# One attention step's products in another order: all attention products first, then all linear products, and x1's rest ahead of the first gated sum

## The chip, the cores and the metric

The kernel runs on one core of one Trainium2 chip. The metric is the time of one execution on the device in microseconds (us); lower is better. The core's engines are TensorE (PE in the rows, PEld its weight loads), VectorE (DVE), ScalarE (ACT), GpSimd (POOL) and SyncE (SP), which issues transfers. Each has its own queue of instructions, and they meet only at semaphores.

## The reference

Two layers over x, 8 x 512 tokens of 256 features, in 32-bit floats. The change is in the first, a gated attention unit. For each of the 8 sequences of 512 tokens:

- x is normed; qk = silu(x Wqk), v = silu(x Wv) (512 wide), gate = silu(x Wg) (512 wide).
- From qk come four sets of heads, turned by position: two queries and two keys.
- **Attention part**: within groups of 64 tokens, att = relu(q k / 64 + bias) squared, and quad_out = att v.
- **Linear part**: kv = k2 v over the whole sequence, divided by 512, and lin_out = q2 kv.
- out = gate * (quad_out + lin_out), then the output projection Wo, a norm, the residual sum with x and another norm: x1.

The second layer is a mixture of eight experts, of which each token uses two, beside a shared one, with a residual sum and a norm.

## The kernel before, in words

**Stages.** `attention` works through the 8 sequences in steps b = 0 to 10; every engine runs the same `step(b)` in its own version. Step b holds the main part of sequence b (`main`), the transposes that prepare sequence b + 1 (`ahead`), the output projection, norm and residual sum of sequence b - 1 (`o`), and the last norm, the transposes and the router logits of sequence b - 2 (`last`). Steps 0, 1 and 2 are written out, 3 to 6 are a loop, the others are written out again. In steps 8 and 9, which have no main part, the first chunks of the shared expert (`beside`) stand between the rest. `experts` follows and takes the other 600 us; it isn't touched.

**The order on TensorE (L735 to L884).** In a main step: the qk product (bank 5) and the v products (banks 0 to 3, of which 1 to 3 wait until VectorE has read the last step's sums, `u_ml`); transposes of the logits (L779); the output projection of sequence b - 1, which waits for `ul_rd` (L791, L709 to L711); transposes of the keys (L801) and the scores (L806); the gate products (banks 0 to 3); the kv product (L826, bank 6); transposes of xn for the next sequence (L716); the wait for `att_rd`; from step 2 on, transposes of x1 into banks 4 and 5 (L716); and then the products of this change, for four quarters m of 128 of the 512 features. Quarter m goes to bank 1 + m and consists of two linear products of 512 columns, kvh times lq (L855) and kvl times lq (L856), and four attention products of 128 columns each, v times att (L859). The first two have their operands in fp32r, the others are plain 32-bit and are recorded as two matmuls each, so a quarter shows two and eight. Ahead of the first quarter TensorE waits for `kvl_rd` (the low part of kv, by VectorE) and `lq_rd` (the low part of the query, moved between partitions by a transfer of SP); ahead of quarter m for the gate of the bank's former content (`g_ev`), ahead of the fourth for ScalarE's copy of the first x1 transposes (`x1T_ev`). Each quarter ends with an increment of `u_mm`. Behind them stand the logits of sequence b - 2 (L877, L878), which wait for `x1l_rd`.

**VectorE.** Its order in a main step: statistics of z and x_in, `moments` (L141 to L147) and `rsqrt` (L129 to L134) on them; the rotated heads (L582 to L589); the residual sum with its bias (L593), statistics of the projection's output, `moments` again (its first instruction is L141), `rsqrt`, the norm of z (L606, L612); the query's low part (L618); att (L625, L630); kvl (L633); the low part of the next x (`xT_rest`, L540); and then the gated sums: for each quarter the product of the gate u with bank 1 + m (L644), and, one quarter behind, `rest(m)`, which is u less ScalarE's rounded copy uh (L639). Behind the first product stands `x1_rest` (L577), two subtractions that make the low part of x1 from ScalarE's x1T and x1h.

**ScalarE** copies and activates: the rounded keys, the gates (L470), kvh (L473), xT (L399) and its rounded copy, x1T and x1h, and the four rounded copies uh (all L390); behind those the copy of the logits' product, lgT (L390), for which the next step's transposes L779 wait. **GpSimd** splits the shared expert's weights in six pieces, one in each of the steps 2 to 7, each released by `o_mm`, which the output projection increments at its end (L379, L384). **SP** issues the transfers in a fixed order, among them the low query (L346) and the stores of x1h and x1l (L350, L352), and in step 8 the loads of the shared expert's first tokens (L326).

Of the kernel before, what the change touches and what calls it, by code (L numbers as in the profile page):

```python
# [32 lines left out]
P = 128  # L33
# [9 lines left out]
KE = E // P  # L43
KH = HID // P
TT = T // P
# [49 lines left out]
class Links:  # L95
# [13 lines left out]
    def at(self, base):  # L109
        self.base, self.k = base, 0  # L110
# [75 lines left out]
def attention(nc, a, shared):  # L186
# [3 lines left out]
    fc_mm, h_ev, hh_rd, hl_rd, pj_mm, bank = (shared[k] for k in ("fc_mm", "h_ev", "hh_rd", "hl_rd", "pj_mm", "bank"))  # L190
    bfc, SHW = shared["bfc"], shared["SHW"]
    XHL, X1D, RES = (shared[k] for k in ("XHL", "X1D", "RES"))
    with ExitStack() as ctx:
# [20 lines left out]
        v = sb("v", [P, TT, E])  # L214
# [4 lines left out]
        att = sb("att", [P, TT, P])  # L219
        kvh, kvl = pair("kv", [P, E])  # L220
        lq = sb("lq", [P, T], F32R)
# [35 lines left out]
        lqh_rd, lql_rd, lq_rd, kvl_rd = (sem(n) for n in ("lin_q_hi_ready", "lin_q_lo_ready", "lin_q_lo_moved", "kv_lo_ready"))  # L257
        kT_mm, kT_ev, sc_mm, att_rd, kv_mm, kv_ev = (sem(n) for n in ("kT_transposed", "kT_ready", "scores_product", "att_ready", "kv_product", "kv_ready"))
        u_mm, u_ml, uh_rd, ul_rd = (sem(n) for n in ("u_product", "u_gated", "uh_ready", "ul_ready"))
# [13 lines left out]
        def stages(b):  # L273

            is_main, ahead = (not is_int(b) or b < B), (not is_int(b) or b < B - 1)
            return is_main, ahead, not is_int(b) or 1 <= b <= B, not is_int(b) or 2 <= b <= B + 1
# [235 lines left out]
        def _(dve):  # L514
# [32 lines left out]
            def beside(*chunks):  # L547

                for j in chunks:
                    dve.wait_ge(hh_rd, j + 1)  # L550
                    tt(e_hl[j % 4], e_h[j % 2], e_hh[j % 4].bitcast(F32), ALU.subtract).then_inc(hl_rd, 1)

            def step(b):
                main, ahead, o, last = stages(b)
# [19 lines left out]
                def x1_rest():  # L574
                    for k in range(KD):
                        dve.wait_ge(x1h_rd, 2 * c + k + 1)
                        tt(x1l[:, k, :], x1T[:, k, :], x1h[:, k, :].bitcast(F32), ALU.subtract).then_inc(x1l_rd, 1)  # L577

                if main:
                    for s in range(2):  # L580
                        dve.wait_ge(q_ev, 4 * b + 2 * s + 2)
                        last_i = tt(qkr[:, s, :], qk[:, s, :], rope[:, s, :], ALU.mult)  # L582
# [7 lines left out]
                if o:  # L590
# [20 lines left out]
                    for t in range(TT):  # L611
                        last_i = stt(z[:, t, :], z[:, t, :], rs[:, TT + t:TT + t + 1], x_res[:, t, :], ALU.mult, ALU.add)  # L612
# [3 lines left out]
                if main:  # L616
# [6 lines left out]
                    for g in range(P // G):  # L623
                        r = slice(g * G, (g + 1) * G)
                        last_i = stt(att[r, :, r], sc[r, :, r], 1.0 / G,  # L625
                                     bias[r, :].rearrange("p (o n) -> p o n", o=1).to_broadcast([G, TT, G]), ALU.mult, ALU.add)
                    link(last_i)
                    for g in range(P // G):
                        r = slice(g * G, (g + 1) * G)
                        last_i = stt(att[r, :, r], att[r, :, r], 0.0, att[r, :, r], ALU.max, ALU.mult)  # L630
# [6 lines left out]
                def rest(m):  # L637
                    dve.wait_ge(uh_rd, 4 * b + m + 1)
                    tt(ul[:, m, :], u[:, m, :], uh[:, m, :].bitcast(F32), ALU.subtract).then_inc(ul_rd, 1)  # L639

                if main:
                    for m in range(KE):
                        dve.wait_ge(u_mm, 4 * b + m + 1)
                        tt(u[:, m, :], u[:, m, :], bank[1 + m][:, :], ALU.mult).then_inc(u_ml, 1)  # L644
                        if m:
                            rest(m - 1)
                        elif last:
                            x1_rest()
                    rest(KE - 1)
                elif at(B + 1):  # L650
                    beside(6)
                    x1_rest()
                    beside(7)
# [30 lines left out]
            for k, c in enumerate((BQ, BK)):  # L684
                link(nc.vector.tensor_scalar(offs[:, k, :], rope[:, 0, :], vec[:, c:c + 1], None, ALU.mult))
                link(stt(offs[:, k, :], rope[:, 1, :], vec[:, c + 1:c + 2], offs[:, k, :], ALU.mult, ALU.add))
            step(0)
            weights_lo(3)
            bias_rows(bo2[0:BR, :], raw_bo[:, :])
            dve.wait_ge(ld_c, 16 * CONSTS)  # L690
            link(nc.vector.tensor_copy(wr_parts[:, :, 0:NE], wr[:, :, :]))
            tt(wr_parts[:, :, NE:], wr[:, :, :], wr_parts[:, :, 0:NE].bitcast(F32), ALU.subtract).then_inc(tab_rd, 1)
            step(1)
            step(2)
            with dve.Fori(3, B - 1) as b:
                link.enter(b, 3, STEP_LINKS)
# [7 lines left out]
        def _(pe):  # L704
            mm, tr = nc.tensor.matmul, nc.tensor.transpose

            def three(o, wh, wl, xh, xl, start, stop):

                mm(o, wh, xl, start=start, stop=False)  # L709
                mm(o, wl, xh, start=False, stop=False)  # L710
                return mm(o, wh, xh, start=False, stop=stop)  # L711
# [37 lines left out]
            def step(b):  # L749
                main, ahead, o, last = stages(b)  # L750
# [4 lines left out]
                if main:  # L755
# [5 lines left out]
                    for k in range(KD):  # L761
                        last_i = three(bank[5][:, :], wqk[0][:, k, :], wqk[1][:, k, :], xTh[:, k, :], xTl[:, k, :], k == 0, k == KD - 1)
# [4 lines left out]
                    for t in range(TT):  # L767
                        if t:
                            need(pe, u_ml, 4 * (b - 1) + t)
                        cols = slice(t * P, (t + 1) * P)  # L770
                        mm(bank[t][:, :], ones2[:, :], bv2[:, :], start=True, stop=False)
                        for k in range(KD):
                            last_i = three(bank[t][:, :], xTh[:, k, cols], xTl[:, k, cols], wv[0][:, k, :], wv[1][:, k, :],
                                           False, k == KD - 1)
                        last_i.then_inc(v_mm, 1)
                if not is_int(b) or b >= 3:
                    pe.wait_ge(lt_ev, b - 2)
                    for t in range(TT):
                        last_i = tr(bank[7][:, t * P:(t + 1) * P], lgT[:, t * P:(t + 1) * P], ident[:, :])  # L779
                    last_i.then_inc(lg_mm, 1)  # L780
                if o:
# [4 lines left out]
                    for t in range(TT):  # L786
                        if t == 2:
                            need(pe, lg_ev, c)
                        cols = slice(t * P, (t + 1) * P)
                        out = bank[6 + t // 2][:, t % 2 * D:t % 2 * D + D]  # L790
                        mm(out, ones2[:, :], bo2[:, :], start=True, stop=False)  # L791
                        for m in range(KE):
                            last_i = three(out, uh[:, m, cols], ul[:, m, cols], wo[0][:, m, :], wo[1][:, m, :], False, m == KE - 1)
# [26 lines left out]
                if main:  # L820
# [4 lines left out]
                    for t in range(TT):  # L825
                        last_i = mm(bank[6][:, :], kT[:, t, :], v[:, t, :], start=t == 0, stop=t == TT - 1)  # L826
# [15 lines left out]
                        pe.wait_ge(x1T_ev, 2 * c)  # L842
                    transposes(x1, (4, 5), x1T_mm)
                if main:
                    pe.wait_ge(kvl_rd, b + 1)
                    pe.wait_ge(lq_rd, 16 * b + 16)
                    for m in range(KE):
                        if m < 3:
                            pe.wait_ge(g_ev, 4 * b + m + 2)
                        elif last:  # L850
                            pe.wait_ge(x1T_ev, 2 * c + 1)
                        rows = slice(m * P, (m + 1) * P)
                        out = bank[1 + m]

                        mm(out[:, :], kvh[:, rows], lq[:, :], start=True, stop=False)  # L855
                        mm(out[:, :], kvl[:, rows], lq[:, :], start=False, stop=False)  # L856
                        for t in range(TT):
                            cols = slice(t * P, (t + 1) * P)
                            last_i = mm(out[:, cols], v[:, t, rows], att[:, t, :], start=False, stop=t == TT - 1)  # L859
                        last_i.then_inc(u_mm, 1)  # L860
                if at(B):
                    beside(2, 3)
                if at(B + 1):
# [2 lines left out]
                if last:  # L866
# [9 lines left out]
                    for k in range(KD):  # L876
                        mm(bank[7][0:2 * NE, :], wr_parts[:, k, :], x1h[:, k, :], start=k == 0, stop=False)  # L877
                        last_i = mm(bank[7][0:NE, :], wr_parts[:, k, 0:NE], x1l[:, k, :], start=False, stop=k == KD - 1)  # L878
# [6 lines left out]
            pe.wait_ge(xn_rest, TT // 2)  # L885
            transposes(xn, (7, 0), xT_mm)
            steps(pe, step, end=B + 3)


# [1033 lines left out]
```

## Time and profile before

| | |
|---|---|
| median of 3 runs | 914.61 us |
| lowest, highest | 913.58, 917.9 us |
| the profiled execution's own time | 913.94 us |
| its span | 912.1 us |
| granted TensorE clock, mean | 0.997 of full speed |
| TensorE, VectorE, ScalarE, GpSimd busy | 97%, 75%, 60%, 29% of the span |

The profile records one execution. Rows of the timeline give the start and the duration of an instruction, or of several alike in a row (x8), which is then the time from the first one's start to the last one's end; matmuls overlap, so that the start of the next is what tells the pace. What stands in brackets at a row's end is the engine's idle time before it and what ended it. Numbers such as L859 are lines of the kernel; for helpers it is the helper's line, so that the tile's name tells which call it is.

### The profile page before, as it was taken

How to read it: one execution, taken by the hardware profiler on the slowest of the kernel's cores; microseconds unless marked ns; L12 is line 12 of the kernel's file. 1: busy time of each engine (PE TensorE's matmuls, PEld its weight loads, DVE VectorE, ACT ScalarE, POOL GpSimd, SP SyncE). 2: the span in 40 equal slices, each digit the busy share in tenths (PEclk: the TensorE clock that was granted, in tenths of full speed). 3: DMA queues.
4: the chain of work that ended last, by engine and by line, in shares of the span. 5: the costliest groups of instructions: out<-in, count | busy, mean ns of one | idle time of the engine just before them, and what ended most of it. 6: DMA issues, size and time to landing. Idle time of an engine off the chain costs nothing.

```text
span 912.1 us, 17238 instructions
## 1 busy us (share of the span) xinstructions
PE 882.9 (97%) x5744; PEld 787.5 (86%) x5744; DVE 682.7 (75%) x1686; ACT 549.7 (60%) x1015; POOL 264.4 (29%) x186
## 2 busy tenths in 40 slices
PE   4999999999999999999999999999999999999995
PEld 3788788788788789899999999999999999999985
DVE  7688889889978599676576675757655579997475
ACT  5546656666646755556556455555545568887475
POOL 0000011001010047338535255543535345542000
PEclk9999999999999999999999999999999999999998
DMA  5142224223226424529665474855676558886723
GB/s 168 52 154 75 85 76 138 75 75 115 75 89 211 170 49 82 134 93 266 151 202 128 152 225 98 248 144 169 152 239 179 145 132 231 230 227 191 239 70 115
DMA packets 70126, 133.35 MB, mean 146 GB/s; under 512 B 14334, under 2 KB 55095, under 8 KB 62776
## 3 DMA queue, kind: packets, MB, share of 16 engines
q1 hardware_dynamic: 49864, 107.68, 35.6%
q0 software_dynamic: 16512, 21.32, 13.9%
q10 hardware_dynamic: 3696, 3.67, 1.2%
q8 instruction: 29, 0.48, 0.2%
q14 instruction: 25, 0.20, 0.1%
HBM read 98.13 MB, written 33.46 MB: 144 GB/s over the span
## 4 chain that ended last, share of the span: by engine, by line
PE 52%; DVE 7%; issue 2%; DMA 2%; ACT 1%; POOL 0%; DVEq 0%; ACTq 0%; SPq 0%; POOLq 0%
PE bank L1719 23%; PE bank L1794 22%; PE bank L1739 3%; PE bank L1745 3%; DVE s_hl L1632 2%; DMA k_wstage<-wall 2%; PE bank L1779 1%; DMA residual_sums<-s_y,s_dest 1%; POOL residual_sums L1178 0%; DVE s_mst L1584 0%; PE bank L1817 0%; DVE s_wpj0l L1529 0%; DVE s_wfc0l L1529 0%; ACT s_h L1314 0%; ACT s_hh L1318 0%
## 5 line engine op out<-in xcount | busy, mean ns | idle before, releaser
L1314 ACT ACTIVATE s_h<-bank,k_bfc 128x512 f32<-128x512 f32 (+1 forms) x216 | 134.4, 622 | 196.4 <-PE bank L1794 187.4
L1632 DVE TENSOR_TENSOR s_hl<-s_h,s_hh 128x512 fp32r<-128x512 f32 (+1 forms) x206 | 124.9, 607 | 133.0 <-ACT s_hh L1318 132.1
L1178 POOL DMA_INDIRECT residual_sums<-s_y,s_dest x64 | 108.5, 1696 | 183.4 <-DVE s_y L1562 170.0
L1318 ACT ACTIVATE s_hh<-s_h 128x512 fp32r<-128x512 f32 (+1 forms) x216 | 122.9, 569 | 9.1
L1794 PE MATMUL bank<-k_uh,s_wfc0h 128*128 128x512 f32 (+1 forms) x384 | 120.2, 361 | 0.0
L1719 PE MATMUL bank<-k_wpj1l,s_hh 128*128 128x256 f32 x384 | 108.6, 283 | 2.1 <-DVE s_hl L1632 2.1
L1719 PE MATMUL bank<-k_wpj1h,s_hh 128*128 128x256 f32 x384 | 108.0, 281 | 0.0
L1719 PE MATMUL bank<-k_wpj1h,s_hl 128*128 128x256 f32 x384 | 107.9, 281 | 0.0
L1719 PE MATMUL bank<-s_wpj0l,s_hh 128*128 128x256 f32 x344 | 96.7, 281 | 0.5 <-DVE s_hl L1632 0.4
L1719 PE MATMUL bank<-s_wpj0h,s_hh 128*128 128x256 f32 x344 | 96.5, 281 | 0.0
L1719 PE MATMUL bank<-s_wpj0h,s_hl 128*128 128x256 f32 x344 | 96.4, 280 | 0.0
L1168 POOL DMA_INDIRECT s_xb<-x_rows,s_token x64 | 71.4, 1115 | 52.2 <-issue 17.7
L1719 PEld LDWEIGHTS bank<-k_wpj1l,s_hh 128*128 128x128 f32 x384 | 72.2, 188 | 6.1 <-DVE s_hl L1632 2.9
L1794 PEld LDWEIGHTS bank<-k_uh,s_wfc0h 128*128 128x128 f32 x384 | 70.1, 188 | 8.5
L1719 PEld LDWEIGHTS bank<-k_wpj1h,s_hl 128*128 128x128 f32 x384 | 72.2, 188 | 3.4
L1719 PEld LDWEIGHTS bank<-k_wpj1h,s_hh 128*128 128x128 f32 x384 | 72.3, 188 | 0.0
L1794 PE MATMUL bank<-k_xTl,k_wfc1h 128*128 128x512 f32 (+1 forms) x192 | 72.2, 376 | 0.0
L1794 PE MATMUL bank<-k_xTh,k_wfc1h 128*128 128x512 f32 (+1 forms) x192 | 68.4, 356 | 0.0
L1794 PE MATMUL bank<-k_uh,s_wfc0l 128*128 128x512 f32 (+1 forms) x192 | 68.3, 356 | 0.0
L1719 PEld LDWEIGHTS bank<-s_wpj0l,s_hh 128*128 128x128 f32 x344 | 64.7, 188 | 4.1 <-DVE s_hl L1632 1.1
L1794 PE MATMUL bank<-k_xTh,k_wfc1l 128*128 128x512 f32 (+1 forms) x192 | 68.0, 354 | 0.0
L1719 PEld LDWEIGHTS bank<-s_wpj0h,s_hl 128*128 128x128 f32 x344 | 65.4, 190 | 2.6
(341 smaller groups left out, 2228.8 us busy)
## 6 DMA issues: line engine op xcount, KB each, us to landing
k_wstage<-wall SPq DMA_DIRECT2D x42, 1024.0 KB, 6.0
s_acc<-wall SPq DMA_DIRECT2D x14, 1024.0 KB, 7.8
s_x_res<-x SPq DMA_DIRECT2D x8, 512.0 KB, 4.7
x_rows<-s_x SPq DMA_DIRECT2D x8, 512.0 KB, 3.6
residual_sums<-s_x SPq DMA_DIRECT2D x8, 512.0 KB, 4.3
x_parts<-s_x1h SPq DMA_DIRECT2D x8, 512.0 KB, 2.6
x_parts<-s_x1l SPq DMA_DIRECT2D x8, 512.0 KB, 3.7
k_uh<-x_parts SPq DMA_DIRECT2D x8, 512.0 KB, 5.6
```

The source lines that it names most:

```text
L1168: pool.indirect_dma_start(xb[i][:, t, :], None, X1D, bass.IndirectOffsetOnAxis(token[:, at:at + 1].bitcast(U32), 0), bounds_check=N - 1).t ...
L1178: pool.indirect_dma_start(RES, bass.IndirectOffsetOnAxis(dest[:, at:at + 1].bitcast(U32), 0), y[:, t, :], None, bounds_check=N + S - 1, co ...
L1314: nc.scalar.activation(h[j % 2][:, cols], b[:, cols], ACT.Gelu_apprx_tanh, bias=bfc[w][:, j:j + 1]).then_inc(h_ev, 1)
L1318: nc.scalar.activation(hh[j % RING][:, cols], h[j % 2][:, cols], ACT.Copy).then_inc(hh_rd, 1)
L1632: tt(hl[j % RING][:, cols], h[j % 2][:, cols], hh[j % RING][:, cols].bitcast(F32), ALU.subtract).then_inc(hl_rd, 1)
L1719: last = mm(o, hs[p][:, cols], wpj[w][ws][:, j, :], start=j == 0 and p == 0 and t % 2 == 0, stop=j == KH - 1 and p == 2, skip_group_check= ...
L1739: last = mm(b[:, c * P:(c + 1) * P], fc_one[:, q, rows], x_one[:, q, :], start=q == 0, stop=q == KD - 1)
L1745: last = mm(b[:, 0:D], h_one[:, c, :], pj_one[:, c, :], start=c == 0, stop=c == KH - 1)
L1779: last = nc.tensor.transpose(b[:, t * P:(t + 1) * P], xb[1 - i][:, t, j * P:(j + 1) * P], ident[:, :])
L1794: last = mm(b[:, cols], wfc[w][ws][:, c, rows_], xs[i][:, c, cols], start=c == 0 and p == 0, stop=c == KD - 1 and p == 2)
```

## The change

On TensorE, the loop over the four quarters becomes two loops. The first issues the attention products of all four, each quarter behind the same wait for its bank as before; the first product into a bank carries the start flag, and the others of the bank write fresh columns. Then come the waits for `kvl_rd` and `lq_rd`, and the second loop issues the two linear products of each quarter on top, with the stop flag and the increment of `u_mm` on the second. On VectorE, `x1_rest` moves from behind the first gated product to ahead of it. The number of instructions is the same, and no transfer is added, removed or put elsewhere in its queue.

```diff
@@ VectorE, the gated sums
                 if main:
+                    if last:
+                        x1_rest()
                     for m in range(KE):
                         dve.wait_ge(u_mm, 4 * b + m + 1)
                         tt(u[:, m, :], u[:, m, :], bank[1 + m][:, :], ALU.mult).then_inc(u_ml, 1)
                         if m:
                             rest(m - 1)
-                        elif last:
-                            x1_rest()
                     rest(KE - 1)
@@ TensorE
                 if main:
-                    pe.wait_ge(kvl_rd, b + 1)
-                    pe.wait_ge(lq_rd, 16 * b + 16)
                     for m in range(KE):
                         if m < 3:
                             pe.wait_ge(g_ev, 4 * b + m + 2)
                         elif last:
                             pe.wait_ge(x1T_ev, 2 * c + 1)
                         rows = slice(m * P, (m + 1) * P)
-                        out = bank[1 + m]
-
-                        mm(out[:, :], kvh[:, rows], lq[:, :], start=True, stop=False)
-                        mm(out[:, :], kvl[:, rows], lq[:, :], start=False, stop=False)
                         for t in range(TT):
                             cols = slice(t * P, (t + 1) * P)
-                            last_i = mm(out[:, cols], v[:, t, rows], att[:, t, :], start=False, stop=t == TT - 1)
-                        last_i.then_inc(u_mm, 1)
+                            mm(bank[1 + m][:, cols], v[:, t, rows], att[:, t, :], start=t == 0, stop=False, skip_group_check=True)
+                    pe.wait_ge(kvl_rd, b + 1)
+                    pe.wait_ge(lq_rd, 16 * b + 16)
+                    for m in range(KE):
+                        rows = slice(m * P, (m + 1) * P)
+                        mm(bank[1 + m][:, :], kvh[:, rows], lq[:, :], start=False, stop=False, skip_group_check=True)
+                        mm(bank[1 + m][:, :], kvl[:, rows], lq[:, :], start=False, stop=True, skip_group_check=True).then_inc(u_mm, 1)
```

## Rows read from the trace of the kernel before

**Rows 1.** The page, busy time, share of the span and instructions of each engine.
```profile
PE 882.9 (97%) x5744; PEld 787.5 (86%) x5744; DVE 682.7 (75%) x1686; ACT 549.7 (60%) x1015; POOL 264.4 (29%) x186
```

**Rows 2.** Busy time by window: stretch, length, PE, PEld, DVE, ACT, POOL, clock, DMA.
```profile
134.90:168.35 33.45, 33.45 (x196) 27.64 (x195) 30.05 (x82) 20.98 (x38) 2.36 (x1) 1.00 0.31 98
...
276.20:311.50 35.30, 34.01 (x232) 30.31 (x232) 24.49 (x91) 21.78 (x39) 0.00 (x0) 1.00 0.58 194
```

**Rows 3.** The timeline of TensorE in step 4, from the x1 transposes on.
```profile
167.46 1.04 PE L716 MATMUL bank<-k_ident,s_x 128*128 128x128 f32 x8
168.36 0.47 PE L855 MATMUL bank<-s_lq,s_kvh 128*128 128x512 f32 x1
168.66 0.39 PE L856 MATMUL bank<-s_lq,s_kvl 128*128 128x512 f32 x1
168.89 1.05 PE L859 MATMUL bank<-s_att,s_v 128*128 128x128 f32 x8
169.70 0.48 PE L855 MATMUL bank<-s_lq,s_kvh 128*128 128x512 f32 x1
```

**Rows 4.** The timeline of TensorE ahead of the products in steps 0 and 1.
```profile
37.45 0.47 PE L855 MATMUL bank<-s_lq,s_kvh 128*128 128x512 f32 x1 [0.58 <-issue]
...
67.78 1.04 PE L716 MATMUL bank<-k_ident,s_xn 128*128 128x128 f32 x8
...
69.40 0.47 PE L855 MATMUL bank<-s_lq,s_kvh 128*128 128x512 f32 x1 [0.58 <-issue]
```

**Rows 5.** The timeline of VectorE: step 0's fourth gated product, step 1's att and kvl.
```profile
43.13 0.69 DVE L644 TENSOR_TENSOR s_u<-s_u,bank 128x512 f32<-128x512 f32 x1
...
66.58 0.85 DVE L630 SCALAR_TENSOR_TENSOR s_att<-s_att 64x256 f32<-64x256 f32 x2
68.60 0.69 DVE L633 SCALAR_TENSOR_TENSOR s_kvl<-bank,s_kvh 128x512 fp32r<-128x512 f32 x1 [1.17 <-ACT s_kvh L473]
```

**Rows 6.** The timeline of step 7's end and step 8's begin, three engines.
```profile
267.66 1.09 PE L716 MATMUL bank<-k_ident,s_x 128*128 128x128 f32 x8 [0.56 <-DVE s_att L630]
...
270.17 0.69 DVE L644 TENSOR_TENSOR s_u<-s_u,bank 128x512 f32<-128x512 f32 x1 [1.71 <-PE bank L859]
...
274.38 0.68 DVE L644 TENSOR_TENSOR s_u<-s_u,bank 128x512 f32<-128x512 f32 x1
274.98 1.47 DVE L639 TENSOR_TENSOR s_ul<-s_u,k_uh 128x512 fp32r<-128x512 f32 x2
...
275.10 0.63 ACT L390 ACTIVATE k_uh<-s_u 128x512 fp32r<-128x512 f32 x1 [0.57 <-DVE s_u L644]
...
276.25 0.66 PE L779 MATMUL bank<-k_ident,s_lgT 128*128 128x128 f32 x4 [1.13 <-ACT s_lgT L390]
```

**Rows 7.** The timeline of VectorE and GpSimd in step 4.
```profile
153.75 1.22 DVE L593 TENSOR_TENSOR s_x_res<-s_x_res,s_ln 128x1024 f32<-128x1024 f32 x1
...
156.08 2.36 POOL L384 TENSOR_TENSOR k_wfc1l<-k_wstage,k_wfc1h 128x1024 fp32r<-128x1024 f32 x1 [31.02 <-PE bank L711]
...
156.83 1.63 DVE L141 TENSOR_TENSOR s_mean<-s_st 128x4 f32<-128x4 f32 x1
...
166.39 0.85 DVE L630 SCALAR_TENSOR_TENSOR s_att<-s_att 64x256 f32<-64x256 f32 x2
...
174.90 0.68 DVE L644 TENSOR_TENSOR s_u<-s_u,bank 128x512 f32<-128x512 f32 x1
```

**Rows 8.** The timeline of GpSimd, VectorE and TensorE in step 2.
```profile
89.34 1.90 POOL L379 TENSOR_SCALAR k_wfc1h<-k_wstage 128x2048 fp32r<-128x2048 f32 x1 [86.90 <-PE bank L711]
...
87.17 1.22 DVE L593 TENSOR_TENSOR s_x_res<-s_x_res,s_ln 128x1024 f32<-128x1024 f32 x1
...
89.98 1.26 DVE L141 TENSOR_TENSOR s_mean<-s_st 128x4 f32<-128x4 f32 x1
...
99.17 0.85 DVE L630 SCALAR_TENSOR_TENSOR s_att<-s_att 64x256 f32<-64x256 f32 x2
...
100.61 1.04 PE L716 MATMUL bank<-k_ident,s_x 128*128 128x128 f32 x8
```

## The prediction, made before the changed kernel was run

> **What bounds the kernel now.** I read the page first, for the engine that fills the span; then the busy time in windows cut at each attention step, to see whether that engine has idle time where the change is made; then TensorE's instructions in order of time through the stretch that is reordered, and the other engines' instructions on either side of it. The page gives TensorE 97% of the span [rows 1]. The windows sharpen that: the stretch from step 3's products to step 4's (a step is one pass b, counted from 0), 134.90 to 168.35, holds 33.45 us of TensorE work in 33.45 us, at a granted clock of 1.00, which is the 2.4 GHz level; VectorE has 30.05 and ScalarE 20.98 in it. The stretch behind the last product step, 276.20 to 311.50, holds 34.01 of TensorE in 35.30 [rows 2]. So in the middle steps nothing can be won by taking a wait of TensorE away, because there is none; the reader should see at once that the change can only pay in steps with a hole.
>
> **The order itself costs nothing.** One quarter is two linear products and four attention products, the latter recorded as eight (two records each). In step 4 it begins at 168.36, the second linear product at 168.66, the eight records at 168.89, the next quarter at 169.70: 1.34 us, of which 0.23 is a linear product in full stream and 0.81 the eight records [rows 3]. The change issues the same 8 linear products and 32 records, 5.4 us, in another order. The 0.30 instead of 0.23 behind the first linear product looks like a price of changing from 4-byte to fp32r products, three of which would go. But the eight records and eight transposes of the same size last the same from first start to last end, 1.05 and 1.04 [rows 3], while the linear product behind the records is entered 0.81 after their start and the one behind the transposes 0.90 (167.46 to 168.36) [rows 3]. So the 0.07 that seems lost behind the change is gained, as 0.09, ahead of it: the start of the first linear product is recorded early. Bounds: a gain of 3 x 0.07 x 8 steps = 1.7 us, or 0; I take 0, because both halves stand in the same rows.
>
> **What is won: two holes.** Steps 0 and 1 have no x1 transposes between the transposes of xn and the products. There TensorE is free 0.9 behind the start of the transposes, at 67.78 + 0.9 = 68.7, and starts at 69.40 [rows 4], just behind VectorE's kvl, 68.60 + 0.69 = 69.29 [rows 5]. Now the attention products, which need neither kvl nor the moved lq, stand first. Step 0 shows the same idle time, 0.58 by the profile's reckoning of ends, before its 37.45 [rows 4]; so TensorE enters step 1 about 0.7 earlier.
>
> **What is lost: the gated sums start late.** VectorE's first gated product waits for u_mm. Before, it came 1.65 after the start T of the products (step 7: T = 267.66 + 0.9 = 268.5, product at 270.17 [rows 6]), that is 0.3 behind the first quarter's 1.34. After, the first u_mm comes only when all but three linear pairs are out: 5.4 - 3 x 0.46 = 4.0, so VectorE starts at T + 4.3. Behind that stand two products (each 0.60 from start to start [rows 6]), then rest(0), which waits for ScalarE's rounded copy of quarter 0: 0.68 + 0.63 + about 0.07 of signalling behind the product's start [rows 6] puts it 0.18 later than VectorE is free. The fourth product therefore starts at T + 4.3 + 0.6 + 0.78 + 3 x 0.6 = T + 7.5. Moving x1's rest forward puts it into this wait: its two instructions of some 0.6 each depend on ScalarE's x1h, which isn't moved, and run there instead of between the first product and the second, where they would now add 1.2 to the lag. So this part costs 0; if x1h came later than T + 3, it would push the chain by what is missing. The parts x1l go out by SP a little earlier, and the loads queued behind them on SP with them; no queue is passed by a new transfer.
> In step 4, T + 7.5 is 175.84, where the fourth product now starts at 174.90 [rows 7]. VectorE enters each following step about 0.9 us late, and TensorE doesn't. Who meets this?
>
> Step 1: VectorE comes in late by 37.45 - 0.7 + 7.5 - 43.13 = 1.1 [rows 4, 5], has no idle time on its way, and finishes att at 66.58 + 0.85 + 1.1 = 68.5 [rows 5]. TensorE starts the products there, 68.55 with the signal, not at 68.7 - 0.7 = 68.0. Against 69.40 it has won 0.85 in all so far.
>
> Step 2: TensorE reaches the end of the output projection at 89.34 - 0.85 = 88.49, where GpSimd starts its split of the weights (1.90 us). VectorE's residual sum L593 runs, 0.93 late, from 88.1 to 89.3 [rows 8]. Today VectorE's L141, an instruction on four columns, lasts 1.26 and ends with GpSimd's 1.90 us instruction: 89.98 + 1.26 = 91.24 = 89.34 + 1.90 [rows 8], and in step 4 1.63, ending at 158.46 against 158.44 [rows 7]. So it waits for GpSimd. What GpSimd does when VectorE is in first, no row shows. Bounds: it runs beside it, L141 is free when VectorE gets there, and att is 0.17 sooner than now; or it is held until 89.3, ends at 91.2, and att stands where it does now, at 99.17 + 0.85 = 100.02 [rows 8]. I take the second, since the wait in [rows 7, 8] holds for a whole instruction. TensorE, ready for the x1 transposes at 100.61 - 0.85 = 99.76, then waits until 100.07: 0.54 of the gain is left (0.7 by the other bound).
> The Trainium skill (SBUF — State Buffer, Who interferes with whom) says that a VectorE instruction with two SBUF inputs and a GpSimd one that reads SBUF exclude each other, whichever started first holding the port to its end. The two stretched L141 agree; by it the gain after step 2 is the 0.54, else 0.7.
>
> Steps 3 to 6: here the stretched L141 is a cushion. In step 4 VectorE gets to it at 156.83 and is let go at 158.4; arriving 0.94 later, at 157.8 at most, it is let go at the same time [rows 7]. L593, at 153.75 + 0.94 = 154.69 until 155.9, is done before GpSimd starts at 156.08. So att stays at 166.39 + 0.85 = 167.24 against TensorE's 167.46 [rows 3, 7], and these four steps cost 0 and win 0. If the cushion weren't there, each would cost 0.94 less the slack of 0.22: 0.7.
>
> Step 7: the same cushion holds; TensorE's wait for att, 0.56, remains [rows 6].
>
> Step 8: no projections stand between the last products and the output projection. TensorE's next instruction there, the transposes of the logits at 276.25, waits for ScalarE's copy of them, which stands behind the four rounded copies [rows 6]. They hang on the fourth gated product: now 274.38, then 268.5 + 7.5 = 276.0. That is 1.6 us later on a path that TensorE fills from there to 311.5 [rows 2]. Bounds: 1.6, or 0.3 less, since the stretch has 1.3 us of holes and some may take a part. I take 1.6.
>
> **Sum.** -0.7 in step 0, -0.15 in step 1, +0.31 in step 2, 0 in steps 3 to 7, +1.6 at step 8: +1.1 us. The profiled execution took 913.94 (span 912.1), so it would take 915.0. It lies 0.67 under the median shown, 914.61; on that the forecast is 915.7. A measurement of this kernel can tell some 0.5%, 4.6 us, from no change; this is a quarter of it.
>
> **Rivals.**
> A. The late end is absorbed, or the gain at the changes of type is real: the loss at step 8 meets the holes behind it or the start of the expert stage, and -0.5 to -1.5 is left, 913.6. For it: 1.3 us of holes in the last window. Against: TensorE is the waiting engine at 276.25 and dense behind it. Chance 0.20.
> B. Slower, by the port between VectorE and GpSimd in steps 3 to 7: if VectorE comes out of the gated sums more than 1.1 us late, L593 is still running when GpSimd's turn comes, GpSimd is held and with it L141; or the cushion just moves along. Then att is late by 0.7 past TensorE's slack in four steps and 0.9 in step 7, which has no slack: +3.7, with the sum 919.4. It decides at a lag of 1.1 (L593's end against 156.08 [rows 7]); I have 0.94, so 0.2 is all there is. Against it: step 4's numbers leave VectorE 0.6 us before L141 is let go. Chance 0.10.
> C. Thirty-two 4-byte products in a row run slower than eight, because each loads fresh weights. The page has 787.5 us for 5744 loads, 0.137 each [rows 1], against 0.11 a record; if the records fell to that, 32 x 0.027 x 8 steps = +7 us, 922. Against: eight in a row last no longer than eight transposes [rows 3]. Chance 0.03.
> D. The change does nothing that counts: kvl isn't what holds steps 0 and 1, and the end is hidden, 914.6. Chance 0.07.
> The forecast has 0.60.
>
> **How the numbers follow.** 915.7 is the likeliest case. The range goes down to case A with all of both holes kept, 914.6 - 1.5, less the 1.0 by which the lowest run (913.58) lies under the median: 912.1; and up to the forecast with 0.5 us of slip in each of four or five steps: 918.1. B in full and C are left out, 0.13, and a little on the low side. Faster by over 0.5% needs 4.6 us, three times what all holes hold: 0.03. Slower by as much is most of B, and C: 0.10. The rest, 0.87, is within 0.5%.
>
> **What the profile after would show.** TensorE without idle time before the first product in step 0 (start near 36.8), a first product at about 68.5 in step 1 with att as its releaser; 32 records in 3.5 to 3.6 us; VectorE's fourth gated product 7.5 behind T; att in step 4 still 0.2 ahead of the x1 transposes, with L141 shorter than 1.63 by about 0.5; the transposes of the logits in step 8 near 277.3. Wrong would be: TensorE waiting for att in steps 3 to 6 (B), records at more than 0.115 (C), or the logits' transposes at or before 276.3 (A).

## The result and the profile after

| | before | after |
|---|---|---|
| median, 22 runs each | 915.68 us | 916.94 us |
| lowest, highest | 913.58, 917.9 | 915.69, 919.68 |
| the profiled execution's own time, its span | 913.94, 912.1 | 916.29, 914.5 |
| granted TensorE clock, mean | 0.997 | 0.996 |

The ratio is 1.0017, 95% interval [1.0011, 1.0022]: slower by 1.3 us. That is below what the prediction calls a difference (0.5%) and the two ranges overlap, but the interval leaves out 1: with 22 runs each the medians tell it. The median of before was 914.61 with the three runs that the prediction was made from; with 22 it is 915.68.

The page's busy line of the kernel after, against [rows 1]; TensorE has the same 5744 instructions:
```profile
PE 884.0 (97%) x5744; PEld 787.6 (86%) x5744; DVE 679.9 (74%) x1686; ACT 549.2 (60%) x1015; POOL 265.4 (29%) x186
```

TensorE in order of time, steps 0 and 1, against [rows 4]; L853 are the attention products, L858 the linear ones:
```profile
36.65 1.04 PE L716 MATMUL bank<-k_ident,s_xn 128*128 128x128 f32 x8
37.53 3.74 PE L853 MATMUL bank<-s_att,s_v 128*128 128x128 f32 x32
41.02 0.48 PE L858 MATMUL bank<-s_lq,s_kvh 128*128 128x512 f32 x1
...
56.92 0.28 PE L711 MATMUL bank<-s_woh,k_uh 128*128 128x256 f32 x1
57.28 0.63 PE L801 MATMUL bank<-k_ident,s_heads 128*128 128x128 f32 x4
...
68.07 1.04 PE L716 MATMUL bank<-k_ident,s_xn 128*128 128x128 f32 x8
69.30 1.94 PE L853 MATMUL bank<-s_att,s_v 128*128 128x128 f32 x15 [0.20 <-DVE s_att L630]
```
The products of step 0 follow the transposes by 0.88, without the 0.58 of idle time of [rows 4]. In step 1 the releaser is att; before, the products started just behind kvl (69.29), and the moved lq was there by then: its transfer was issued at 65.7 and landed 2.3 us later. New is the gap ahead of 57.28: the keys' transposes start 0.36 behind the last output product instead of 0.12, and VectorE's first finished heads (L588, 56.38 + 0.75 = 57.13) stand just ahead of them.

GpSimd and VectorE in step 2, against [rows 8]:
```profile
89.28 2.62 POOL L379 TENSOR_SCALAR k_wfc1h<-k_wstage 128x2048 fp32r<-128x2048 f32 x1 [86.85 <-PE bank L711]
```
```profile
88.90 1.22 DVE L593 TENSOR_TENSOR s_x_res<-s_x_res,s_ln 128x1024 f32<-128x1024 f32 x1
90.04 1.42 DVE L531 BATCH_NORM_STATS2 s_st<-bank 128x6 f32<-128x256 f32 x4
91.49 0.41 DVE L141 TENSOR_TENSOR s_mean<-s_st 128x4 f32<-128x4 f32 x1
```
VectorE's residual sum is in first this time (88.90), and GpSimd's copy, 1.90 before, takes 2.62: it is held until about 90.0, where the sum ends, and then has its 1.9. L141 ends at 91.90, with GpSimd.

VectorE in step 4, against [rows 7], and TensorE there, against [rows 3]:
```profile
157.36 1.20 DVE L141 TENSOR_TENSOR s_mean<-s_st 128x4 f32<-128x4 f32 x1
...
166.48 0.85 DVE L630 SCALAR_TENSOR_TENSOR s_att<-s_att 64x256 f32<-64x256 f32 x2
...
171.38 1.29 DVE L577 TENSOR_TENSOR s_x1l<-s_x1T,s_x1h 128x512 fp32r<-128x512 f32 x2 [0.72 <-ACT s_x1h L390]
172.66 1.28 DVE L646 TENSOR_TENSOR s_u<-s_u,bank 128x512 f32<-128x512 f32 x2
...
175.86 0.68 DVE L646 TENSOR_TENSOR s_u<-s_u,bank 128x512 f32<-128x512 f32 x1
```
```profile
167.56 1.04 PE L716 MATMUL bank<-k_ident,s_x 128*128 128x128 f32 x8
168.43 3.74 PE L853 MATMUL bank<-s_att,s_v 128*128 128x128 f32 x32
171.92 0.47 PE L858 MATMUL bank<-s_lq,s_kvh 128*128 128x512 f32 x1
...
173.85 0.40 PE L876 MATMUL bank<-s_x1h,s_wr_parts 128*16 128x512 f32 x1
```
Thirty-two attention records take 3.49 us from the first's start to the linear product, 0.109 each; from one start to the next it is 0.112, against 0.111 in before. The fourth gated product starts at T + 7.43 (T = 168.43). VectorE enters L141 0.53 later than before, and is let go at 158.56, with GpSimd's piece as before; att comes 0.09 later and the x1 transposes wait for nothing. x1's rest fits into the wait for the first u_mm, but only just: it waits for x1h until T + 2.95, ends at T + 4.24, and the first gated product starts at T + 4.23, where it starts in step 0 too (37.53 to 41.77), which has no x1's rest.

Step 8, ScalarE, then TensorE, against [rows 6]:
```profile
276.63 0.63 ACT L390 ACTIVATE k_uh<-s_u 128x512 fp32r<-128x512 f32 x1 [0.57 <-DVE s_u L646]
277.17 0.57 ACT L390 ACTIVATE s_lgT<-bank 16x512 f32<-16x512 f32 x1
```
```profile
274.60 0.40 PE L877 MATMUL bank<-s_x1l,s_wr_parts 128*8 128x512 f32 x1
277.79 0.66 PE L779 MATMUL bank<-k_ident,s_lgT 128*128 128x128 f32 x4 [2.79 <-ACT s_lgT L390]
```
The rounded copy of the fourth quarter starts at 276.63 instead of 275.10, the copy of the logits behind it, and the logits' transposes at 277.79 instead of 276.25. TensorE is idle for 2.79 us instead of 1.13.

To see where the time goes, the start of the same TensorE instruction is compared between two profiles. The time up to step 0's transposes differs between executions by up to 1.7 us, whatever the kernel, so shifts count from there: the shift of those transposes themselves (+0.83 in after, -0.34 in e7, -0.41 in e9) is taken off. In us against before:

| up to | after | e7, the change again | e9, the change once more |
|---|---|---|---|
| products of step 0 done | -0.81 | -0.80 | -0.79 |
| behind the keys' transposes of step 1 | -0.54 | -0.53 | -0.53 |
| products of step 1 done | -0.88 | -0.87 | -0.89 |
| end of step 2 | -0.66 | -0.65 | -0.61 |
| x1 transposes of step 7 | -0.94 | -0.93 | -0.89 |
| logits' transposes of step 8 | +0.71 | +0.73 | +0.76 |
| six us later | +0.70 | +2.25 | +2.30 |
| end of the attention stage | +0.70 | +2.25 | +2.28 |

All three have the same pattern up to the logits' transposes. Behind them two have lost another 1.5 us. The forecast has no such term.

### The profile page after: what moved, and what is told of

Same layout as the page of the kernel before. It is cut to its first block, busy times and chain, and to the rows that moved or that the text cites. A ratio compares the mean times of both kernels' runs of the same rounds, so it can differ in the third digit from the quotient of the medians.

```text
span 914.5 us, 17234 instructions
## 1 busy us (share of the span) xinstructions
PE 884.0 (97%) x5744; PEld 787.6 (86%) x5744; DVE 679.9 (74%) x1686; ACT 549.2 (60%) x1015; POOL 265.4 (29%) x186
## 4 chain that ended last, share of the span: by engine, by line
PE 57%; DVE 4%; DMA 2%; ACT 1%; issue 1%; ACTq 0%; DVEq 0%; SPq 0%
PE bank L1718 25%; PE bank L1793 25%; PE bank L1738 3%; PE bank L1744 3%; DMA k_wstage<-wall 2%; PE bank L1778 1%; DVE s_hl L1631 1%; DVE s_mst L1583 0%; PE bank L1816 0%; ACT s_h L1313 0%; ACT s_hh L1317 0%; PE bank L1835 0%; ACT s_acc L1334 0%; DVE s_mtmp L133 0%; DVE s_mrs L134 0%
```

## The experiments

**e1: where does the loss at the end come from?** The change stays in every step but step 7 (B - 1), whose code on both engines is that of before.
```diff
-                if main:
+                if main and not at(B - 1):
                     for m in range(KE):
...
+                elif main:
+                    pe.wait_ge(kvl_rd, b + 1)
+                    pe.wait_ge(lq_rd, 16 * b + 16)
+                    for m in range(KE):
...
```


> The change everywhere but in step 7, which keeps the order of before on TensorE and VectorE. My theory: the change wins about 0.8 us in the first steps and loses 1.6 at the begin of step 8, because step 7's fourth gated product comes late and nothing covers that. Then this kernel loses nothing at step 8: its transposes of the logits stand as far behind step 7's x1 transposes as before (8.6 us, against 10.2 with the change), and the time is 0.5 to 1.0 us below before, 1.6 below the change. Rival, that the loss is spread or lies in the expert stage: the time stays 1 to 1.5 above before.

Measured: 914.65 against 915.22 (27 runs), ratio 0.9991 [0.9982, 1.0]. From step 0's transposes to the end of the attention stage it is 0.89 us shorter than before; the logits' transposes wait 1.13 again. The whole loss of 1.65 sits in step 7's order. Without it the stage is shorter than before; in the medians that is 0.6 us, and their interval just reaches 1.

**e2: is x1's rest free where it was?** The new order on TensorE, x1's rest left behind the first gated product.
```diff
-                    if last:
-                        x1_rest()
                     for m in range(KE):
...
                         if m:
                             rest(m - 1)
+                        elif last:
+                            x1_rest()
```


> TensorE's new order, but x1's rest stays behind the first gated product on VectorE. My theory: x1's rest adds 1.2 us to VectorE's lag, which becomes 1.8 in steps 3 to 7. Now L593 is running when GpSimd's turn comes in steps 3, 4 and 6, GpSimd's piece is held for about 0.6 and lengthened by it, L141 is let go 0.6 later and TensorE waits for att about 0.4 in each of these steps; at step 8 the loss is 2.6 instead of 1.6. In all 2.5 to 3 us over before. Rival, that the port isn't handed over so: no wait in steps 3 to 6, and 1.3 to 1.8 over before by the last step alone. Rival, that x1's rest is free wherever it stands: as the change, 1.3 over before.

Measured: 924.1 against 915.22, ratio 1.0096 [1.0082, 1.0111], 8.9 us, three times what was expected. TensorE in steps 4, 7 and 8:
```profile
175.62 0.40 PE L876 MATMUL bank<-s_x1h,s_wr_parts 128*16 128x512 f32 x1 [0.68 <-DVE s_x1l L577]
...
278.12 0.41 PE L876 MATMUL bank<-s_x1h,s_wr_parts 128*16 128x512 f32 x1 [0.61 <-DVE s_x1l L577]
...
282.26 1.12 PE L779 MATMUL bank<-k_ident,s_lgT 128*128 128x128 f32 x4 [3.04 <-ACT s_lgT L390]
```
VectorE in step 4:
```profile
173.60 0.69 DVE L644 TENSOR_TENSOR s_u<-s_u,bank 128x512 f32<-128x512 f32 x1 [2.00 <-PE bank L859]
174.20 1.28 DVE L577 TENSOR_TENSOR s_x1l<-s_x1T,s_x1h 128x512 fp32r<-128x512 f32 x2
```
The expectation looked at VectorE's lag and forgot a reader: TensorE's logits products stand right behind the linear ones and wait for x1l. With x1's rest at 174.20 TensorE stands idle for 0.68 ahead of them in step 4, and for 0.61 to 0.68 in each of steps 2 to 7: counted as in the table, the shift is -0.88 behind step 1 and +0.17 behind step 2, grows by 0.77 in each step from there, and is +3.25 at step 7's x1 transposes. The transposes of step 8 add 2.67, and then the clock fell:
```profile
278.00:282.00 4.00, 1.10 (x4) 0.29 (x4) 3.90 (x8) 2.16 (x4) 0.00 (x0) 1.00 0.34 133
282.00:285.00 3.00, 2.74 (x13) 2.74 (x14) 2.83 (x14) 0.43 (x2) 0.00 (x0) 0.52 0.83 250
```
(Columns as in [rows 2]: after VectorE, ScalarE and GpSimd stands the granted clock.) Behind four us with 1.10 of TensorE work it was granted 0.52, the 1.2 GHz level, and 1.5 us went there. So the stage is 7.4 us longer in this profile. Another 1.9 go at the start of the experts, where the clock fell a second time (0.72 as the mean from 328 to 334).

**e3: x1's rest ahead, TensorE's order old.**
```diff
                 if main:
+                    if last:
+                        x1_rest()
                     for m in range(KE):
...
-                        elif last:
-                            x1_rest()
```


> Only x1's rest moved ahead of the first gated product, TensorE's order as before. My theory: VectorE's fourth gated product is 0.8 later in steps 2 to 6, where the wait for GpSimd's piece absorbs it, and not later in step 7, where it has to wait for TensorE's last quarter; the time is within 0.3 us of before. Rival, that the moved rest is the part that costs: 1 us or more over before.

Measured: 915.25 against 915.22, ratio 1.0 [0.9991, 1.001]; the shift stays between +0.63 and +0.69 from step 0 to step 8, so the stage has the same length within 0.06. By itself the move does nothing; with the new order it is what brings the cost down from 8.9 us to the 1.3 to 1.7 of the change.

**e4 and e10: the order of each quarter alone.** Attention products first within a quarter, then its two linear ones; the waits for kvl and lq behind the first quarter's attention products; VectorE as before. The edit is against before, and the old products that it replaces are left out.
```diff
-                    pe.wait_ge(kvl_rd, b + 1)
-                    pe.wait_ge(lq_rd, 16 * b + 16)
                     for m in range(KE):
...
+                        for t in range(TT):
+                            cols = slice(t * P, (t + 1) * P)
+                            mm(bank[1 + m][:, cols], v[:, t, rows], att[:, t, :], start=t == 0, stop=False, skip_group_check=True)
+                        if m == 0:
+                            pe.wait_ge(kvl_rd, b + 1)
+                            pe.wait_ge(lq_rd, 16 * b + 16)
+                        mm(bank[1 + m][:, :], kvh[:, rows], lq[:, :], start=False, stop=False, skip_group_check=True)
+                        mm(bank[1 + m][:, :], kvl[:, rows], lq[:, :], start=False, stop=True, skip_group_check=True).then_inc(u_mm, 1)
```


> Neither whole order: in each quarter the attention products come first and the linear ones behind them, u_mm after each quarter as before, and the waits for kvl and lq stand behind the first quarter's attention products; VectorE as before. My theory: 0.9 us of attention products cover the hole of 0.75 in steps 0 and 1 as well as four quarters of them do, and the gated sums start no later, so nothing is lost: TensorE 0.75 earlier after step 0, 1.5 after step 1, and so to the end, 1.2 to 1.6 us below before. Rival, that the holes come back as waits for VectorE: about as before.

> The version of e4 again, to have its time twice. If e4's ratio of 0.9984 holds: 1 to 2 us under before, ratio 0.998 to 0.999, attention stage 2.0 us shorter from step 0 to step 8, granted clock 1.00 in step 8, since its wait for the logits' copies stays near the 1.1 us of before. If e4's time was chance: 0.0 to 0.5 under before.

Measured: 914.32 against 915.22, ratio 0.9984 [0.9974, 0.9994], and again 914.02 against 915.16, ratio 0.9984 [0.9975, 0.9993]. TensorE in e4, step 1 and step 7:
```profile
67.45 1.04 PE L716 MATMUL bank<-k_ident,s_xn 128*128 128x128 f32 x8
68.32 1.06 PE L853 MATMUL bank<-s_att,s_v 128*128 128x128 f32 x8
69.14 0.47 PE L857 MATMUL bank<-s_lq,s_kvh 128*128 128x512 f32 x1
...
272.24 0.39 PE L858 MATMUL bank<-s_lq,s_kvl 128*128 128x512 f32 x1
...
274.71 0.66 PE L779 MATMUL bank<-k_ident,s_lgT 128*128 128x128 f32 x4 [1.15 <-ACT s_lgT L390]
```
Both holes are closed in full (-0.82 in step 0, -0.82 in step 1, no wait for att), the gated sums are not late, and the transposes of step 8 wait the old 1.15. The attention stage is 2.05 and 2.06 us shorter in the two profiles. This version beats both kernels, before by 0.9 and 1.1 us in the medians. Some of its gain is gone where the experts start: from the end of the attention stage to 400 us the shift grew by 1.9 in one profile and 1.0 in the other.

**e5 and e6: the change in steps 0 and 1 alone, and in step 7 alone.** The diff is that of e1 with another condition, `is_int(b) and b < 2` and `at(B - 1)`.

> The change in steps 0 and 1 alone, the order of before from step 2 on (x1's rest does not exist in steps 0 and 1). My theory: the whole gain of the change is made here and part of it is given back in step 2, where VectorE comes late and holds GpSimd's piece: TensorE 0.75 earlier into step 1, about 0.6 earlier from step 2's x1 transposes on, then the same to the end, since the steps behind keep their order and nothing is late at step 8. The time is 0.4 to 0.8 below before, and GpSimd's first piece lasts 2.6 instead of 1.9. Rival, that step 2's late VectorE eats all of it: as before.

> The change in step 7 alone, the order of before in all others. My theory: the whole loss is here: the transposes of the logits in step 8 stand 10.2 us behind step 7's x1 transposes instead of 8.6, all else is as before, and the time is 1.6 us over before (1.2 to 2.0). Rival, that the loss needs the lag of the earlier steps as well: within 0.5 of before.

Measured: e5 914.74 against 915.57 (26 runs), ratio 0.9993 [0.9985, 1.0002], stage 0.62 shorter. e6 917.99, ratio 1.0029 [1.0019, 1.0039]: 2.4 us, where 1.6 were expected. Its profile has the expected 1.65 up to the logits' transposes, and another 1.53 behind them. Busy time and granted clock of TensorE in e6; the last three columns are the clock, the DMA share and GB/s:
```profile
276.00:278.00 2.00, 0.05 (x1) 0.05 (x1) 1.91 (x4) 1.33 (x3) 0.00 (x0) 1.00 0.82 213
278.00:280.00 2.00, 2.00 (x12) 2.00 (x13) 1.93 (x10) 0.22 (x1) 0.00 (x0) 0.60 0.96 378
280.00:282.00 2.00, 2.00 (x12) 2.00 (x12) 1.66 (x13) 0.00 (x0) 0.00 (x0) 0.55 0.53 187
282.00:284.00 2.00, 2.00 (x19) 2.00 (x18) 1.90 (x6) 1.22 (x3) 0.00 (x0) 1.00 0.00 0
```
In two us twelve products of the output projection instead of nineteen: the clock fell to 0.55 to 0.60 in these slices, behind the longer idle stretch.

**e7 and e9: the change again,** unaltered, to see how often.

> The changed kernel once more, for a second profile beside the first: the two hundredths-exact shifts against before in the attention stage (about -0.7 after step 0's start, -0.06 in each step from 3 on, +1.65 at step 8) should come again, while the time before step 0's first transposes and the expert stage, where my theory has no part, should differ between two executions by several tenths. If the expert stage is again 0.8 us longer than in the profile of before, the change lengthens it and my sum lacks a term. Time 1.0 to 1.6 over before.

> The change once more, one look at the clock. Theory 1: like after and e7, the attention stage is 0.7 longer than before's from step 0 to step 8, plus 1.5 if the granted clock falls behind step 8's idle stretch (2.8 us), nothing if not; so either +0.7 or +2.2 at the time of before's 309.8 us, taken from step 0's start. Theory 2 (the fall is rare): +0.7.

Measured: e7 917.31, ratio 1.002 [1.0011, 1.0029]; e9, one run with a profile, 916.82. The table above has their shifts. TensorE in e9:
```profile
276.61 0.66 PE L779 MATMUL bank<-k_ident,s_lgT 128*128 128x128 f32 x4 [2.81 <-ACT s_lgT L390]
...
277.23 0.30 PE L709 MATMUL bank<-s_wol,k_uh 128*128 128x256 f32 x1
277.35 0.39 PE L710 MATMUL bank<-s_woh,s_ul 128*128 128x256 f32 x1
277.54 0.41 PE L711 MATMUL bank<-s_woh,k_uh 128*128 128x256 f32 x1
```
Within four instructions a product goes from 0.28 or 0.30 to 0.41, and from 0.12 to 0.21 from start to start, and stays there for some 3 us. Of four profiles with an idle stretch of 2.8 us in step 8 (after, e6, e7, e9) three have the fall, and e2's with 3.04 has it; of six with one of 1.1 (before, e1, e3, e4, e5, e10) none.

The runs without a profile say something too, since each has its mean granted clock on record. It is 0.9958 over 75 runs of before, 0.9950 over the 35 of the change (after, e7, e9) and 0.9944 over the eight of e6. In e7 the mean of the six us behind the idle stretch (276.6 to 282.6) is 0.72, which is 1.7 us of full clock, or 0.0018 of the kernel. The change's 0.0008 less is then some 0.4 falls more per execution than before, an estimate. The means don't say where in the kernel they lie, and other places count too: e5, whose step 8 is that of before, has 0.9972 over twelve runs.

**e8: fill the stretch.** The change, with ten more products ahead of step 8's wait, into a bank that nobody reads.
```diff
+                if at(B):
+                    for _ in range(10):
+                        mm(bank[5][:, :], kvh[:, 0:P], lq[:, :], start=True, stop=True)
                 if not is_int(b) or b >= 3:
                     pe.wait_ge(lt_ev, b - 2)
```


> The change everywhere, with ten more 128x512 products into bank 5 (nobody reads them) ahead of step 8's wait for the logits' transposed copies: 10 x 0.23 = 2.3 us of the 2.8 us in which TensorE is idle there. Theory 1 (a second cost of the change is the clock: e6 and e7 showed the granted clock at 0.5 to 0.6 for about 3 us behind a 2.8 us idle stretch, which added 1.53 us, after's own profile did not): the granted clock stays 1.00 between 274 and 284 in the profile, step 8's shift against before stays at about +1.65 over step 7's, and the median comes out some 0.5 to 1 us under that of the change, 0.3 to 1.0 us over before. Theory 2 (the fall has another cause than the idle stretch, or costs nothing in the end): the clock falls here too, or the median stays 1.5 to 1.7 over before. The filler itself should add nothing, as the wait for the copies ends 0.5 us behind it; if the logits' bank were disturbed, the transposes would start over 2.9 us behind the logits.

Measured: 916.09 against 915.16 (22 runs), ratio 1.0009 [1.0, 1.0018]. TensorE:
```profile
273.25 2.44 PE L778 MATMUL bank<-s_lq,s_kvh 128*128 128x512 f32 x10
276.21 0.66 PE L782 MATMUL bank<-k_ident,s_lgT 128*128 128x128 f32 x4 [0.52 <-ACT s_lgT L390]
```
The transposes come at the same place in the pattern (+1.65), the clock stays at 1.00 from 270 to 312, and the stage ends at +0.78 instead of +2.25. The 1.5 us behind the transposes is gone. One profile is weak evidence for that, as the first one of the change had no fall either. The medians point that way: e8 is over before by 0.9, the change by 1.3 (22 runs) and 1.7 (e7); but the intervals of e8 and e7 overlap ([1.0, 1.0018] and [1.0011, 1.0029]). The mean granted clock points that way too: over e8's eleven runs it is 0.9957, as in before, and not the change's 0.9950. Profiles, medians and means together make the idle stretch the likely cause; none shows it alone.

## Why the prediction was right, and where it was not

The forecast was 1.1 over before; 1.3 was measured (1.7 in e7). The mechanism is right: a gain in steps 0 and 1, a part of it given back in step 2, nothing in steps 3 to 6 and a loss at step 8. That the size of the whole fits as well is partly luck. The attention stage by itself came out 0.7 longer; the missing 0.35 is mostly the order's own gain (0.28), taken as 0, and a smaller loss in step 2 (0.09). A term that the sum didn't have, the clock, made up for them. The absolute forecast, 915.7 against 916.94 measured, is low for another reason: it stands on the median of three runs of before, which was 1.1 under that of 22.

**The order itself, 0 of bounds 0 and 1.7.** Not quite: TensorE gains 0.07 in each of steps 3 to 6, 0.28 in all where the text took 0. Rival C fell: thirty-two records in a row have the pace of eight (0.112 against 0.111). The gain doesn't go by the number of changes between 4-byte and fp32r products: e4 saves one pair of them per step, the change four, and e4 gains as much, 0.09 in each of the same steps. What both share is that attention products follow transposes directly; which part of that pays wasn't tried.

**Step 0, -0.7, and step 1, -0.15.** Measured -0.80, and -0.88 for both. One reader of the lag was left out between them: the keys' transposes of step 1 wait for VectorE's heads and give 0.27 back (57.28). It cost nothing in the end, since step 1's products wait for att, which hangs on the same VectorE chain and not on TensorE: att is their releaser, as forecast, and the gain of 0.85 came out as 0.88.

**Step 2, +0.31 by the bound in which GpSimd is held.** This was the choice between two bounds that no row showed. GpSimd's 2.62 instead of 1.90 decides it: an engine that comes second waits, whichever it is. The price was +0.22 to +0.28, forecast as 0.31. The Trainium skill (SBUF — State Buffer, Who interferes with whom) says that VectorE's instruction with two SBUF inputs and GpSimd's that reads SBUF exclude each other; the traces agree in both directions, with 1.20 for an L141 that is held and 2.62 for a GpSimd copy that is held. The four statistics that read a PSUM bank (L531) run beside it undisturbed, 1.42 against 1.41 in step 1, where GpSimd has no piece.

**Steps 3 to 6, 0, and rival B.** Right. L141 is let go at 158.56 although VectorE comes 0.53 later (the text said up to 0.94; the statistics ahead of it had waited 0.40 for TensorE before, and don't any more). L593 ends at 154.77 + 1.22 = 155.99, only 0.2 before GpSimd's 156.18, the margin that the text named. No wait for att appears.

**x1's rest moved "costs 0".** True, and the text under-told it: it priced the old place as 1.2 on VectorE's lag. The larger price is TensorE's, since the logits' products wait for x1l, 0.77 per step (e2).

**Step 8, +1.6.** 1.65 in all five profiles that have step 7's new order and x1's rest ahead (after, e6 to e9). The fourth product came at T + 7.4, not 7.5. The transposes of the logits, forecast "near 277.3", came at 277.79, or 276.96 without the 0.83 of this execution's later start. Nothing was absorbed: rival A fell.

**What failed: that the sum ends there.** The idle stretch grew from 1.13 to 2.79, and in three of four profiles the granted clock fell behind it, for 1.5 us. The stage is 0.7 longer without the fall and 2.25 with it. The medians, +1.3 and +1.7, lie between. By the mean granted clocks it falls some 0.4 times more per execution than before; at 1.5 us each that is 0.6, and with the stage's 0.7 makes 1.3, an estimate that fits. The text gave the idle time only as a delay and never asked what TensorE's clock does behind it.

Open stays the start of the experts' stage. From the end of the attention stage to 400 us the shift changes by -0.1 (after) to +1.9 (e4, e2), in kernels with the change and without it. In e2, e4, e6, e8, e9 and e10 the clock fell there too, to 0.72 as the mean of the six us that hold the fall, each time within 1.3 us behind an idle stretch of TensorE of 1.9 to 2.0 us; in the other six profiles it didn't, behind stretches as long. How long TensorE stands idle there, and what decides on the fall, wasn't tested.

## What to carry to other kernels

Price an order by who waits for its first and its last result: here the gain (TensorE doesn't wait for kvl) needed only the first quarter's attention products ahead, and putting all four there delayed every gated sum. When an engine's queue is reordered, list each reader of each tile that now comes late, the engine's own later instructions among them. And where a wait of TensorE grows, as from 1.13 to 2.79 us here, look at the granted clock behind it in several profiles, not in one: it may cost a second time.

## What the runs showed of the hardware

- TensorE's granted clock fell from 1.00 to between 0.50 and 0.60 (the 1.2 GHz level, in slices where it may have changed within) behind step 8's idle stretches of 2.80, 2.81, 2.81 and 3.04 us in dense work (e6, e7, e9, e2), and not behind one of 2.79 (after), 1.12 to 1.15 (six profiles) or 0.52 (e8). Slower products began with the first instruction in e2, 0.4 us behind it in e6, and 0.7 and 1.0 in e9 and e7; they lasted 3 to 4 us, which cost 1.5. At the start of the experts' stage the clock also fell behind idle stretches of 1.9 to 2.0 us, in six of the twelve profiles. So the length of the stretch doesn't decide alone; what else does is open. That a stretch brings it on is supported by e8, its profile and its eleven runs.
- GpSimd and VectorE hold each other off in both directions: 1.90 to 2.62 for GpSimd's copy when VectorE's sum was in first by 0.4 us, and 1.20 to 1.63 for VectorE's L141, 0.17 by itself, when GpSimd was in first.
- The start-up until the first transposes differed by 1.7 us between executions (-0.84 to +0.83), as much as the effects measured here; single spans can't be compared without taking it off.
